# Spreading the first tile's routing roots with TensorE instead of a DMA, with the first step of the order rewritten

## The reference

```
x = x + retention(layernorm(x)) @ Wo      # 8 heads of 16, chunks of 64, state carried over chunks
z = layernorm(x)
probs = softmax(z @ Wg)                   # 8 experts
top_w, top_i = top_k(probs, 2);  top_w /= sum(top_w) + 1e-8
h = square(relu(z @ W1[e]))               # 128 -> 256, for every expert e
out = x + sum_e combine[:, e] * (h @ W2[e])
```

## Time and profile before

| | us |
|---|---|
| median of 3 runs (lowest, highest) | 279.1 (278.1, 279.32) |
| time of the profiled execution | 280.09 |
| its span, first to last instruction | 278.2 |
| TensorE busy in the span | 267.4 (96%) |
| GpSimd busy | 210.8 (76%) |
| VectorE busy | 202.5 (73%) |
| ScalarE busy | 184.9 (66%) |

### The profile page before, as it was taken

One profiled execution on the slowest core, in us unless ns is written; L12 is line 12 of the kernel. 1 busy time (PEld: TensorE's weight loads), 2 busy tenths in 40 slices (PEclk: granted clock), 3 DMA queues, 4 the chain that ended last, 5 costly groups with the idle time before them and its releaser, 6 DMA issues.

```text
span 278.2 us, 8908 instructions
## 1 busy us (share of the span) xinstructions
PE 267.4 (96%) x3614; PEld 209.3 (75%) x3614; DVE 202.5 (73%) x489; ACT 184.9 (66%) x306; POOL 210.8 (76%) x221
## 2 busy tenths in 40 slices
PE   7999979998999999999999999999999999999995
PEld 5565657677887788778887788778887788788883
DVE  2778348984959986595758866595857679898783
ACT  2566538919794588675794578675794677777871
POOL 2235885999999988987989878988889848744452
PEclk9999999999999999999999999999999999999999
DMA  7328255205250251413350250104320251144202
GB/s 220 130 64 272 75 153 155 75 4 154 78 151 5 79 190 39 115 53 112 108 152 4 80 185 12 73 5 146 123 75 2 80 174 33 64 154 117 72 0 75
DMA packets 13592, 26.85 MB, mean 97 GB/s; under 512 B 1136, under 2 KB 6512, under 8 KB 13552
## 3 DMA queue, kind: packets, MB, share of 16 engines
q1 hardware_dynamic: 13552, 26.30, 30.0%
HBM read 24.07 MB, written 2.23 MB: 95 GB/s over the span
## 4 chain that ended last, share of the span: by engine, by line
PE 68%; POOL 10%; issue 10%; DVE 5%; DMA 2%; ACT 2%; POOLq 1%; DVEq 0%
POOL act_lo L1134 9%; PE h_ps L346 8%; PE y_ps L367 7%; PE y_ps L361 7%; PE h_ps L348 7%; PE h_ps L347 7%; PE y_ps L362 7%; PE bank L501 4%; PE bank L435 2%; PE bank L513 2%; PE bank L523 2%; PE bank L465 2%; DVE act_s L766 2%; PE bank L486 2%; PE y_ps L325 1%
## 5 line engine op out<-in xcount | busy, mean ns | idle before, releaser
L1134 POOL TENSOR_TENSOR act_lo<-act_f,act_hi 128x512 fp32r<-128x512 f32 x112 | 144.0, 1309 | 39.8 <-ACT act_f L976 39.4
L766 DVE SCALAR_TENSOR_TENSOR act_s<-h_ps,scale 128x1024 f32<-128x1024 f32 x64 | 77.7, 1216 | 26.9 <-issue 14.7
L971 ACT ACTIVATE act_hi<-act_s 128x1024 fp32r<-128x1024 f32 x64 | 68.5, 1071 | 24.4 <-DVE act_s L766 24.2
L976 ACT ACTIVATE act_f<-act_s 128x1024 f32<-128x1024 f32 x64 | 67.8, 1060 | 1.0 <-POOL act_lo L1134 1.0
L346 PE MATMUL h_ps<-x_hi,w_lo 128*128 128x512 f32 x128 | 53.3, 416 | 2.1 <-DVE act_s L766 2.1
L361 PE MATMUL y_ps<-act_hi,w_lo 128*128 128x512 f32 x128 | 52.5, 410 | 0.0
L348 PE MATMUL h_ps<-x_hi,w_hi 128*128 128x512 f32 x128 | 50.7, 396 | 0.0
L362 PE MATMUL y_ps<-act_hi,w_hi 128*128 128x512 f32 x128 | 50.5, 394 | 0.0
L347 PE MATMUL h_ps<-x_lo,w_hi 128*128 128x512 f32 x128 | 50.5, 394 | 0.0
L367 PE MATMUL y_ps<-act_lo,w_hi 128*128 128x512 f32 x128 | 40.4, 397 | 1.0 <-POOL act_lo L1134 0.9
L346 PEld LDWEIGHTS h_ps<-x_hi,w_lo 128*128 128x128 f32 x128 | 24.1, 188 | 9.7 <-DVE act_s L766 2.9
(11 more groups left out here) (123 smaller groups left out, 384.6 us busy)
## 6 DMA issues: line engine op xcount, KB each, us to landing
scale<-scratch SPq DMA_DIRECT2D x32, 512.0 KB, 4.2
x_t_in<-x_tr SPq DMA_DIRECT2D x8, 256.0 KB, 4.9
x_all<-x SPq DMA_DIRECT2D x8, 256.0 KB, 4.8
out<-out_sb SPq DMA_DIRECT2D x8, 256.0 KB, 4.0
scale<-w SPq DMA_DIRECT2D x2, 256.0 KB, 4.5
scale<-w SPq DMA_DIRECT2D x1, 512.0 KB, 4.2
cst<-constants SPq DMA_DIRECT2D x1, 417.0 KB, 5.2
cst<-constants SPq DMA_DIRECT2D x1, 296.0 KB, 5.4
```

Source lines behind the costliest of these rows:

```text
L766: nc.vector.scalar_tensor_tensor(out=act_s[:, u % 2], in0=h_ps[:, u % 2], scalar=0.0, in1=scale[:, f % 2, e].unsqueeze(1).to_broadcast([P, ...
L971: nc.scalar.activation(act_hi[:, u % 4], act_s[:, u % 2], ACT.Square).then_inc(act_hi_ready, 1)
L976: nc.scalar.activation(act_f[:, u % 2], act_s[:, u % 2], ACT.Square).then_inc(act_f_ready, 1)
L1134: nc.gpsimd.tensor_tensor(act_lo[:, u % 4, n], act_f[:, u % 2, n], act_hi[:, u % 4, n].bitcast(F32), ALU.subtract).then_inc(pool_low_ready, 1)
```

## The change

For experts 0 and 1 of tile 0 the roots no longer pass through memory. A new helper `roots_beside(e)` makes four matmuls whose stationary operand is one column of `combine_r`, repeated 128 times along the free axis, and whose moving operand is the identity: each partition of `y_ps` then holds the roots of 128 tokens. ScalarE copies `y_ps` to `scale[:, 0, e]` (`copy_beside`), and `scale_h` of units 0 and 1 waits for this copy instead of a load. The load of quarter 0 of tile 0 is gone; `quarter_loads` counts the loads that there are, for the waits. `transpose_roots(0)` and its store stay, since the other three quarters are loaded as before; its result lies in `bank0` now.

With it the lists of step 0 change. On TensorE the seven matmuls of zeros are gone, `project_k(2)` stands behind the second half of `outputs_within(1)`, first products 2 and 3 stand between the steps of tile 1's output, and `w2_product(0)` and `w2_product(1)` stand ahead of and behind `project_v(2)`, so nothing is left between `scores(2)` and `w1_product(0, 5)`. On ScalarE the squares of units 0 and 1 stand ahead of `mask_q(2)` and `high_x(1)`. On VectorE `scale_h` of units 0 and 1 stands ahead of `decay_k(2)` and `add_attention(1)`. On GpSimd `low(1)` stands ahead of `root_variance(1, 1)`, and `root_variance(2, 0)` stands behind `low(2)`.

```diff
@@ SyncE @@
             store_roots(0)
-            load_scale(0, 0)
             load_scale(0, 1)
@@ TensorE, helpers @@
             def w2_product(u):
                 if u == 0:
+                    pe.wait_ge(beside_ready, PER_PART)
...
             def project_k(s):
                 elif s == 2:
-                    pe.wait_ge(piece_whole, PIECES)
+                    pe.wait_ge(root_t_ready, 1)
...
+            def roots_beside(e):
+
+                if e == 0:
                     pe.wait_ge(piece_whole, PIECES - 1)
                 else:
+                    pe.wait_ge(beside_ready, e)
+                for g in range(GROUPS):
+                    last = pe.matmul(y_ps[:, P * g:P * (g + 1)], combine_r[:, e, g:g + 1].to_broadcast([P, P]), ident,
+                                     start=True, stop=True)
+                last.then_inc(beside_done, 1)
@@ TensorE, list @@
             w1_product(0, 0)
             outputs_within(1, (0, 1))
+            transpose_roots(0)
+            roots_beside(0)
+            w1_product(0, 1)
+            roots_beside(1)
+            outputs_within(1, (2, 3))
             project_k(2)
-            transpose_roots(0)
-            w1_product(0, 1)
-            outputs_within(1, (2, 3))
             outputs_before(1)
             transpose_k(2)
-            pe.wait_ge(root_t_ready, 1)
-            keep_warm(3)
+            w1_product(0, 2)
             project_out(1)
-            keep_warm(4)
+            w1_product(0, 3)
             transpose_x2(1)
             project_q(2)
-            w1_product(0, 2)
-            w1_product(0, 3)
             w1_product(0, 4)
+            w2_product(0)
             project_v(2)
-            w2_product(0)
+            w2_product(1)
@@ VectorE @@
             def scale_h(f, e):
-                if e % PER_PART == 0:
-                    dve.wait_ge(scale_loaded[f % 2][e // PER_PART], DMA * (f // 2 + 1))
+                if f == 0 and e < PER_PART:
+                    dve.wait_ge(beside_ready, e + 1)
+                elif e % PER_PART == 0:
+                    dve.wait_ge(scale_loaded[f % 2][e // PER_PART], DMA * quarter_loads(f, e // PER_PART))
...
-            decay_k(2)
-            add_attention(1)
             for f in range(TILES):
...
                 if f == 0:
                     scale_h(f, 1)
+                    decay_k(a)
+                    add_attention(p)
                     scale_h(f, 2)
@@ ScalarE @@
+            def copy_beside(e):
+                act.wait_ge(beside_done, e + 1)
+                nc.scalar.copy(scale[:, 0, e], y_ps[:]).then_inc(beside_ready, 1)
...
             copy_roots(0)
+            copy_beside(0)
             high_second()
+            copy_beside(1)
             copy_k(2)
             copy_o(1)
             for f in range(TILES):
                 if f == 0:
+                    square(u)
+                    square(u + 1)
+                    mask_q(a)
                     high_x(p)
-                    square(u)
-                    mask_q(a)
-                    square(u + 1)
                     copy_v(a)
@@ GpSimd @@
             low_second()
-            root_variance(2, 0)
             for f in range(TILES):
                 if f == 0:
                     low(u)
+                    low(u + 1)
                     root_variance(p, 1)
                     shift_logits(p)
-                    low(u + 1)
                     low(u + 2)
+                    root_variance(a, 0)
```

More of the change, by code:

```diff
@@ L171, in out_rows, with quarter_loads @@
             return slice(PW * at, PW * (at + 1))
-        def root_bank(s):
-            return y_ps[:] if s == 0 else bank0[:]
+        def quarter_loads(s, j):
+            return s // 2 + (1 if j or s % 2 else 0)
         def piece_bank(i):
@@ L214, in build @@
             sem("combine_ready"), sem("root_t_done"), sem("root_t_ready"), sem("root_stored"))
+        beside_done, beside_ready = sem("beside_done"), sem("beside_ready")
         scale_loaded = [[sem(f"scale_loaded{i}{j}") for j in range(PARTS)] for i in range(2)]
@@ L262, in store_roots @@
                     for j in range(PARTS):
-                        sp.wait_ge(scale_loaded[s % 2][j], DMA * (s // 2))
+                        if quarter_loads(s - 2, j):
+                            sp.wait_ge(scale_loaded[s % 2][j], DMA * quarter_loads(s - 2, j))
                 sp.dma_start(scratch[s % 2].rearrange("(r p) -> r p", p=P), combine_t[:]).then_inc(root_stored, DMA)
@@ L534, in transpose_roots @@
                 if s == 0:
+                    pe.wait_ge(piece_whole, PIECES)
+                else:
+                    pe.wait_ge(attn_ready, PAIRS * min(s + 2, TILES))
+                pe.transpose(bank0[0:EXPERTS * GROUPS, 0:P], combine_r[:].rearrange("p e g -> p (e g)"),
+                             ident).then_inc(root_t_done, 1)
+            def roots_beside(e):
+                if e == 0:
                     pe.wait_ge(piece_whole, PIECES - 1)
                 else:
-                    pe.wait_ge(attn_ready, PAIRS * min(s + 2, TILES))
-                pe.transpose(root_bank(s)[0:EXPERTS * GROUPS, 0:P], combine_r[:].rearrange("p e g -> p (e g)"),
-                             ident).then_inc(root_t_done, 1)
+                    pe.wait_ge(beside_ready, e)
[3 more added lines that the diff above has]
+                last.then_inc(beside_done, 1)
             def slot(f, n):
@@ L595, in _ @@
             outputs_within(1, (0, 1))
+            transpose_roots(0)
[3 more added lines that the diff above has]
+            outputs_within(1, (2, 3))
             project_k(2)
-            transpose_roots(0)
-            w1_product(0, 1)
-            outputs_within(1, (2, 3))
             outputs_before(1)
             transpose_k(2)
-            pe.wait_ge(root_t_ready, 1)
-            keep_warm(3)
+            w1_product(0, 2)
             project_out(1)
-            keep_warm(4)
+            w1_product(0, 3)
             transpose_x2(1)
             project_q(2)
-            w1_product(0, 2)
-            w1_product(0, 3)
             w1_product(0, 4)
+            w2_product(0)
             project_v(2)
-            w2_product(0)
+            w2_product(1)
             for f in range(TILES):
                 for e in range(EXPERTS):
-                    if EXPERTS * f + e <= LAG:
+                    u = EXPERTS * f + e
+                    if u <= LAG:
                         continue
-                    if EXPERTS * f + e > LAG + 1:
+                    if u > LAG + 1:
                         w1_product(f, e)
                     slot(f, 2 * e)
-                    w2_product(EXPERTS * f + e - LAG)
+                    if u > LAG + 1:
+                        w2_product(u - LAG)
                     slot(f, 2 * e + 1)
@@ L964, in copy_roots @@
                     act.wait_ge(root_stored, DMA * s)
-                nc.scalar.copy(combine_t[:], root_bank(s)[0:EXPERTS * GROUPS, 0:P]).then_inc(root_t_ready, 1)
+                nc.scalar.copy(combine_t[:], bank0[0:EXPERTS * GROUPS, 0:P]).then_inc(root_t_ready, 1)
+            def copy_beside(e):
+                act.wait_ge(beside_done, e + 1)
+                nc.scalar.copy(scale[:, 0, e], y_ps[:]).then_inc(beside_ready, 1)
             def square(u):
```

## The result

The changed kernel takes 281.24 us in the median of four runs, against 279.21 for the kernel before: ratio 1.0093, 95% interval 1.0047 to 1.0138. It is slower, by 0.9%. The forecast was 278.5, its range ended at 280.1. Of the rivals D, the clock, is the nearest. Its 280.4 is close in part by luck: it priced the clock too high, and a second loss that I had not seen came on top. (Ratios in this part leave out executions that are over 1.5% above the fastest of the same kernel; medians and lists of executions do not.)

A forecast was written before the change was run, and what follows sets the result against it. TensorE sets the pace from 64 us, after waiting for GpSimd's `low(4)`. That starts from 50.3 + 11.68 + 1.03 - 0.35 = 62.7 against 63.33, 0.6 us earlier: 279.1 - 0.6 = 278.5 us; range 277.2, and 0.2 below it, to 280.1.

The forecast's parts named there:

- D, the clock: TensorE's 2.4 us wait drops its clock, 3.8 us of work at half pace cost 1.9 us: 280.4 us; chance 0.08.
- last step: Behind `w2_product(4)`'s wait for `low(4)`: the program is as before, TensorE-bound, and keeps the 0.6 us.
- gain of 0.6 us: GpSimd's `low(4)`, TensorE's last wait ahead of 64 us, ends at 62.7 us against 63.33.
- What bounds the kernel: TensorE is busy from 64 to 224 us; what is won ahead is kept; the question is when `low(4)` ends.
- The way to `project_v(2)`: TensorE from `combine_r` at 30.75: 14.8 us of work, so `project_v(2)` starts at 45.6 us, 1.3 us earlier.
- the chain from `low(2)` on: GpSimd from 50.3 us: 11.68 us, plus 1.03 for `root_variance(2, 0)`, less 0.35 for L1081; `low(4)` ends at 62.7.
- the term of L1105: GpSimd instruction, L1081 before the change: 0.35 us less than its 1.39, as VectorE's scan moves off it.
- The wait and the clock: TensorE at `w2_product(4)` waits some 2.4 us for `low(4)`, where it waited 0.9; no clock cost in the sum.
- The base: VectorE idles 1.87 us ahead of L766 for the load of quarter 0; the change removes this wait.

The follow-up runs named there:

- experiment 3: The changed kernel with `root_variance(2, 0)` moved ahead of `low(2)` on GpSimd: median 278.35 us, ratio 1.0012 to the kernel before.
- experiment 2: The changed kernel with eight matmuls of zeros in TensorE's wait for `low(4)`: median 281.3 us, ratio 1.0066 to the kernel before.
- experiment 6: The changed kernel with VectorE's variance by a reduction, against the kernel before: with eight matmuls of zeros 0.9971, later 1.0011; reduction alone 1.0041.

## Why the prediction was wrong

The sum failed in two places. Its last step was "Behind it the program is that of before, TensorE-bound, and the 0.6 us are kept": they were not kept, since 1.08 us went to the clock and 1.27 us to a blocked addition. And its gain of 0.6 us was counted from a wait of VectorE that three other profiles do not have.

- *What bounds the kernel.* Right: GpSimd's `low(4)` ends last in step 0, and what is won or lost by 64 us is kept. Wrong was that the program behind it is that of before, TensorE-bound: at 70.78 us VectorE's addition can be held up for 3.35 us, and there TensorE has no work left to cover it.
- *The way to `project_v(2)`, and on to `low(4)`.* Right within 0.5 us in each term; the stalls that were removed came back as a wait of 2.2 us (2.4 forecast) at the place named. The terms' errors partly cancel: the way to `project_v(2)` was 0.45 us shorter than forecast, the chain from `low(2)` on 0.4 us longer. This 0.4 is the term of L1105. The 0.35 us did come off it in both profiles of the changed kernel, but VectorE's scan did not move off GpSimd's work. It now starts beside `low(3)` and takes 1.23 and 1.24 us for 0.76, until 55.84; L1096, which starts at 55.20, takes 0.67 for 0.24, until 55.87. So 0.35 us were won and 0.43 lost, and the term is nothing, in every profile with `root_variance(2, 0)` between the two low parts. With `low(2)` and `low(3)` joined again (experiment 3) L1105 is back at 1.39 and L1096 at 0.22. This agrees with the rule of the Trainium skill, "SBUF — State Buffer", on the shared port pair, on both sides: the later of the two instructions stands still.
- *The wait and the clock.* This is the first step that failed: the wait was in the sum, its price in clock was not. I had the mechanism as rival D, with the right place, and gave it 0.08, since no row showed what 2.4 us do. It happened in every profile with that wait (three of three), and the mean granted clock of the changed kernel was 0.990 to 0.994 in 14 of its 16 timed executions; the other two have 0.998, as executions of the kernel before have. Experiments 2 and 3 show that it is the wait itself, and the last two runs of experiment 6 show its price by the times. I had priced it at 1.9 us, by the pace of full-width matmuls; it was 1.1, since most of the 3.4 us fell on small matmuls, which lost less than half of their pace (0.79 us for 64 became 1.12). The Trainium skill, "TensorE: Matmul & The Clock Gate", in its section on the HAM clock gate, says that the clock falls after idleness and that activity releases it; the trace agrees, with 0.50 for 3.4 us and 1.00 behind them.
- *The block.* Not among my rivals; the sum had this path at nothing. I had named the port rule, and used it for GpSimd's L1105, but only for instructions of VectorE with two inputs in SBUF, and had not asked where VectorE's own additions would stand beside GpSimd's row of low parts in step 1. By the Trainium skill, "SBUF — State Buffer", in the section on the single rule, an instruction like this addition (`tensor_scalar`) can take the shared pair too, and the block lasts for the one instruction of GpSimd that holds it, here 1.3 us. The 1.25 us of the kernel before agree. The 3.35 us do not: they are more than two such instructions, so VectorE was passed over. That the groups of over 281 us in experiment 2 are this block is inferred from their going with the reduction; no execution of those groups was profiled. Their size does not fit well either: they lie 2.6 and 4.9 us above the lowest group, where this profile's block cost 1.27 us and a slow start costs some 2.
- *The base.* I took the 1.87 us of VectorE from one profile as what the change removes. In three others it is 0. By the two of the unchanged kernel this mis-sized the gain by 1.0 to 1.3 us: the 0.6 us forecast was made of a wait that these do not have.

What stays open: how often quarter 0 lands late; what the groups of over 281 us in experiment 2 are made of; why VectorE is passed over in some executions only; and why the first float32 matmuls of the program run at half pace in some executions (below).

## What to carry to other kernels

A wait that is covered elsewhere is not free on TensorE: removing stalls ahead of a fixed bound gathers them into one, and one long wait can cost the clock where two short ones did not. Fill it, or shorten the chain that ends it (here: an instruction of 1.0 us moved into another engine's wait gave 2.3 us by the medians, with the executions of over 281 us gone too). And before a sum is made on a wait for a DMA, look at it in more than one profile.

## What the runs showed of the hardware

- Waits of TensorE of 1.73 us (before) and 1.26 us (experiment 3) left the clock at 1.00; the wait of 2.17 us was followed by 3.4 us at 0.50, and zeros in its place kept it at 1.00.
- The first four float32 projections took 1.98 us in ten profiles and 3.78 in four, whatever the kernel (one of the four is the kernel before with the reduction). The first product then starts at 29.6 us instead of 27.1 to 28.2. This is some 2 us between executions of one program, and the reason why differences of 0.5% took a dozen executions each.
- A `TENSOR_SCALAR` on 128x4 values took 0.17 to 3.35 us beside GpSimd's work (the changed kernel); a `TENSOR_REDUCE` in its place 0.16 in every tile.
